# Attention stage: the instructions of a step written in another order on four engines

## What is computed

```
xn = layernorm(x)                                    # then ln1
q, k = rope(l2norm(xn @ Wq)), rope(l2norm(xn @ Wk))  # 16 heads of 8
v, clock = xn @ Wv, softplus(xn @ clock_w + clock_b)
gcp = exp(clip(cumsum(-softplus(xn @ gate_w + gate_b)), -60, 50))
p_exp = exp(p - max(p)) * clock;  p_cs = cumsum(p_exp)
q = q * gcp / (p_cs + 1e-8);  k = k / (gcp + 1e-8) * p_exp
out = softmax(causal(q @ k.T / sqrt(8))) @ v @ out_w + out_b
x1 = out + residual
y = x1 + gelu(layernorm(x1) @ mlp_w1 + mlp_b1) @ mlp_w2 + mlp_b2
x = x + layernorm(y)                                 # then the expert of each token is chosen
```

## Time and profile before

| what | value |
|---|---|
| median of three runs (lowest, highest) | 2470.77 us (2466.68, 2477.46) |
| the profiled execution: its time, its span | 2465.03 us, 2463.3 us |
| mean granted clock of TensorE over the span | 0.90 |
| `x2`, once a step: first, last of 16 | at 183.5 us, at 991.1 us |

### The profile page before, as it was taken

The page is one execution under the profiler, slowest core; times in us unless marked ns, Lnnn a source line. Parts: engine busy times, 40 slices in busy tenths (PEclk is TensorE's granted clock), DMA queues, the critical chain, the costliest instruction groups (busy, mean ns, idle before and its releaser), DMA issues. The chain is left out here.

```text
span 2463.3 us, 40082 instructions
## 1 busy us (share of the span) xinstructions
PE 1930.4 (78%) x12634; PEld 980.3 (40%) x12661; DVE 1726.9 (70%) x3563; ACT 1493.2 (61%) x2916; POOL 1102.2 (45%) x702
## 2 busy tenths in 40 slices
PE   3678887777887876199648889899888898775997
PEld 0345454444544443199612223332322222223443
DVE  4655655655656532257608999999999999994875
ACT  1576666666766653077535676666666666535875
POOL 0112111212121101158727788888888888860000
PEclk7899899999999986599878999999999999877998
DMA  3010000000100000122110000000000000003432
GB/s 136 18 31 23 23 23 23 27 23 25 37 23 19 19 14 22 31 64 85 68 39 15 25 22 22 22 21 21 21 21 21 21 30 17 18 9 101 100 82 73
DMA packets 98864, 88.51 MB, mean 36 GB/s; under 512 B 8416, under 2 KB 85392, under 8 KB 98336
## 3 DMA queue, kind: packets, MB, share of 16 engines
q1 hardware_dynamic: 91936, 68.52, 9.7%
q0 software_dynamic: 6784, 18.10, 2.2%
HBM read 38.01 MB, written 27.61 MB: 27 GB/s over the span
## 5 line engine op out<-in xcount | busy, mean ns | idle before, releaser
L1790 POOL TENSOR_TENSOR hc<-h,c_rep 128x1024 f32<-128x1024 f32 x256 | 602.1, 2361 | 179.3 <-DVE h L1772 173.1
L1772 DVE TENSOR_TENSOR_SCAN h<-decay,bank 128x1024 f32<-128x1024 f32 x256 | 585.4, 2287 | 30.3 <-DVE bank L1763 11.2
L1666 ACT ACTIVATE decay<-bank,neg_a_r 128x510 f32<-128x510 f32 x512 | 322.7, 683 | 271.5 <-PE bank L1552 271.3
L1538 PE MATMUL bank<-u_in,sel_rows 32*128 32x512 f32 x1024 | 322.8, 682 | 110.3 <-DVE h L1772 109.0
L1763 DVE TENSOR_TENSOR bank<-bank,b_rep 128x1024 f32<-128x1024 f32 x256 | 309.2, 1208 | 62.4 <-remote 51.9
L1552 PE MATMUL bank<-delta,sel_rows 32*128 32x512 f32 x1024 | 348.0, 684 | 1.5 <-ACT decay L1666 1.5
L662 ACT ACTIVATE es<-bank 128x384 f32<-128x384 f32 x512 | 210.1, 502 | 120.6 <-PE bank L467 120.5
L1011 POOL DMA_INDIRECT rows_in_dram<-row,idx x64 | 66.4, 1037 | 424.5 <-DVE row L954 409.9
L1538 PEld LDWEIGHTS bank<-u_in,sel_rows 32*128 32x128 f32 x1024 | 88.1, 195 | 306.8 <-DVE h L1772 263.9
L442 PE MATMUL bank<-xt,w_a 128*128 128x512 f32 x224 | 138.9, 713 | 70.4 <-DVE rot_b L820 32.5
L1567 PE MATMUL bank<-hc,y_sel 128*32 128x512 f32 x1024 | 151.3, 667 | 0.0
(11 more groups left out here) (334 smaller groups left out, 4185.3 us busy)
## 6 DMA issues: line engine op xcount, KB each, us to landing
r_tw<-r_o_t SPq DMA_DIRECT2D x96, 128.0 KB, 2.3
xvs<-xv SPq DMA_DIRECT2D x16, 512.0 KB, 2.9
xs<-rows_in_dram SPq DMA_DIRECT2D x72, 68.0 KB
w<-in_w_dram SPq DMA_DIRECT2D x2, 2048.0 KB
x_in<-in_x_dram SPq DMA_DIRECT2D x16, 256.0 KB
xlb_dram<-xl SPq DMA_DIRECT2D x16, 256.0 KB
xlb_m<-xlb_dram SPq DMA_DIRECT2D x16, 256.0 KB
x_m<-in_x_dram SPq DMA_DIRECT2D x16, 256.0 KB
```

Of the source, the lines that this page charges most:

```text
L1538: last = pe.matmul(BD[n % 2][:, i * STEP:(i + 1) * STEP], sel[at:at + 32, r, :], u_in[p if n < NS else q][at:at + 32, hf, :], start=True, ...
L1666: act.activation(decay[n % 4][:, i, :, 1:], seq(DL[i])[:, :, 1:], ACT.Exp, scale=c["neg_a_r"][:, hf, g:g + 1]).then_inc(s["n_da"], 1)
L1772: dve.tensor_tensor_scan(flat(h[n % RING]), decay[n % 4].rearrange("p i b t -> p (i b t)"), BD[n % 2], 0.0, ALU.mult, ALU.add).then_inc(s[ ...
L1790: pool.tensor_tensor(hc[n % RING][:, :, :], h[n % RING][:, :, :], c_rep[p][:, :].unsqueeze(1).to_broadcast([P, 2, STEP]), ALU.mult).then_i ...
```

## The change

Everything is in `attention`. No operation is added or taken out, no size and no buffer is changed, and the loop stays as it is. `stats_of`, `root`, `turned`, `heads_out` and `chain` are taken apart, so that their pieces (`bn_stats`, `bn_aggr`, `heads_rec`, `heads_o`, single activations) can stand in different places; and between the pieces now stand operations of other parts. Where two operations stood next to each other in an order that made one wait enough, the second now has its own (`f_rq` ahead of `q_t`, `f_pre0` ahead of the Abs, `r_hot` ahead of `pos`, `f_clip` ahead of `factor`).

The diff of `pe_step`, shortened:

```diff
+            if late:
+                weigh(5, k - 2, p)
+            if tail:
+                pe.wait_ge(s["m_h"], k - 2)
+                transposes(M, h_tok, s["m_ht"])
             if front:
                 pe.wait_ge(s["f_xt_sb"], k + 1)
                 since(pe, s["f_mk"], k)
                 project(FB, c["w_gate"], s["f_gate"])
             if tail:
-                pe.wait_ge(s["m_h"], k - 2)
-                transposes(M, h_tok, s["m_ht"])
+                pe.wait_ge(s["m_ht_sb"], k - 2)
+                up(0)
...
+            if late:
+                quad(6, k - 2, p)
...
             if late:
-                weigh(5, k - 2, p)
-            if tail:
-                up(3)
-
-            if late:
-                quad(6, k - 2, p)
+                back(2, k - 2)
...
+            if late:
+                back(3, k - 2)
+            if front:
+                pe.wait_ge(s["f_sq"], k + 1)
+                pe.wait_ge(s["f_ra"], k + 1)
+                pe.matmul(FA[:, :], c["ones_blk"], square[:, :], start=True, stop=True).then_inc(s["f_ssq"], 1)
+                pe.wait_ge(s["f_rb"], k + 1)
+                project(FB, c["w_k"], s["f_k"])
             if ln:
                 pe.wait_ge(s["f_xn"], k + 2)
...
             if scores:
+                weigh(3, k - 1, q)
+                quad(5, k - 1, q)
                 back(1, k - 1)
-                quad(5, k - 1, q)
```

On ACT `h_t` now comes ahead of `v_a`, `av_copy(2)` and the Abs stand between the gelus, the root of `f_vv` comes right behind the second table load, the Exp of `mag` and what follows from it come behind `exps(7)`, and `lnorm` and `neg` stand earlier or later by one group. On DVE and POOL:

```diff
-            def heads_out(i, u, par):
+            def heads_rec(i, u):
+                dve.wait_ge(s["s_tr"], u * 4 + i + 1)
+                dve.reciprocal(rec[:, :, :], AV.rearrange("q (n s w) -> q n s w", n=4, s=HS)[:, :, :, DH]).then_inc(s["s_rec"], 1)
...
+            def heads_o(i, u, par):
...
+                dve.wait_ge(s["s_rec"], u * 4 + i + 1)
...
-            if front:
-                pool.wait_ge(s["f_nb"], k + 1)
-            if tail:
+                pool.wait_ge(s["f_rs"], k + 1)
+                since(pool, s["xlb_stored"], 16 * k)
+                pool.tensor_tensor(xl[:, :, :], x_in[p][:, :, :], of_tile(mv[p][:, :, 0]), ALU.subtract).then_inc(s["f_xl"], 1)
...
-                pool.wait_ge(s["f_xl2"], k + 1)
-                pool.tensor_tensor(xl[:, :, :], xl[:, :, :], c["rows"][:, 0:1, :].to_broadcast([P, TS, D]), ALU.add).then_inc(s["f_xlb"], 1)
...
+            if front:
+                pool.wait_ge(s["f_xl2"], k + 1)
+                pool.tensor_tensor(xl[:, :, :], xl[:, :, :], c["rows"][:, 0:1, :].to_broadcast([P, TS, D]), ALU.add).then_inc(s["f_xlb"], 1)
```

More of the change, by code:

```diff
@@ L393, in since @@
                 eng.wait_ge(sem, count)
[L395 to L405, removed]
         def two_variances(dve, v, var, sem):
@@ L592, in pe_step @@
                 last.then_inc(s["m_aff"], 1)
+            if scores:
+                back(0, k - 1)
             if front:
@@ L597, in pe_step @@
             if scores:
-                weigh(2, k - 1, q)
-            if scores:
-                weigh(3, k - 1, q)
+                quad(3, k - 1, q)
             if mid:
@@ L624, in pe_step @@
                 last.then_inc(s["r_rank"], 1)
+            if scores:
+                weigh(2, k - 1, q)
+                quad(4, k - 1, q)
             if mid:
@@ L668, in av_copy, with gelu @@
                 act.activation(avs[:, :], AV[:, :], ACT.Copy).then_inc(s["s_avs"], 1)
+            def gelu(n):
+                act.wait_ge(s["m_up"], 4 * k + (n - 11))
+                act.activation(g[:, n, :], M[:, :], ACT.Gelu, bias=c["mlp_b1"][:, n:n + 1]).then_inc(s["m_gelu"], 1)
+            if tail:
+                act.wait_ge(s["m_ht"], k - 2)
+                since(act, s["m_up"], 4 * k - 12)
+                act.activation(h_t[:, :], M[:, :], ACT.Identity, scale=c["ln2_g"], bias=c["ln2_b"]).then_inc(s["m_ht_sb"], 1)
             if scores:
@@ L739, in act_step @@
                 exps(1, k - 1)
-            if tail:
-                root(vv_m[:, :, :], vv_m[:, :, :], row[q][:, :, RS0:RS1 + 1].rearrange("p j v -> p v j"), s["m_vv3"], s["m_ln3"], s["m_rs3"], k - 2)
             if front:
-                act.wait_ge(s["f_clip"], k + 1)
-                since(act, s["f_zk"], k)
-                act.activation(lgcp[:, :], cum[:, :], ACT.Exp, scale=-1.0).then_inc(s["f_gcp"], 1)
-                act.wait_ge(s["f_gcp"], k + 1)
-                act.activation(lgcp[:, :], lgcp[:, :], ACT.Ln, bias=1e-8).then_inc(s["f_lgcp"], 1)
-            if scores:
-                exps(2, k - 1)
-                av_copy(0, k - 1)
+                act.wait_ge(s["f_k"], k + 1)
+                act.wait_ge(s["f_ssq"], k + 1)
+                act.activation(square[:, :], FB[:, :], ACT.Square).then_inc(s["f_sk"], 1)
             if tail:
@@ L812, in heads_out, with bn_stats, bn_aggr @@
                     dve.tensor_tensor(o, tr[:, :, r, :, 0:DH], w, ALU.mult).then_inc(s["s_o"], 1)
-            def turned(to, bank, bank_sw, s_a, wait_a, s_b, wait_b, s_r, part):
-                if part == 0:
-                    dve.wait_ge(wait_a, k + 1)
-                    dve.tensor_tensor(seq(to), seq(bank), cos, ALU.mult).then_inc(s_a, 1)
-                    return
-                dve.wait_ge(wait_b, k + 1)
-                dve.tensor_tensor(seq(rot_b), seq(bank_sw), sin, ALU.mult).then_inc(s_b, 1)
-                dve.wait_ge(s_b, k + 1)
-                dve.tensor_tensor(to[:, :], to[:, :], rot_b[:, :], ALU.add).then_inc(s_r, 1)
+            def bn_stats(to, src, sem):
+                for j in range(TS):
+                    last = dve.bn_stats(to[:, j, :], src[:, j, :])
+                last.then_inc(sem, 1)
+            def bn_aggr(to, st, sem):
+                dve.memset(hold[:, :], 0.0)
+                for j in range(TS):
+                    last = dve.bn_aggr(to[:, j, :], st[:, j, :])
+                last.then_inc(sem, 1)
             def centred(dst, src, mean_var, rstd, sem):
@@ L839, in dve_step @@
                 centred(h_tok, x1, mv_m, rs_m, s["m_h"])
+            if ln:
+                dve.wait_ge(x_loaded[q], 16 * half + 16 * (1 + p))
+                since(dve, s["f_xl"], k)
+                bn_stats(stats, x_in[q], s["f_st"])
+                dve.wait_ge(s["f_st"], k + 2)
+                bn_aggr(mv[q], stats, s["f_mv"])
             if front:
```

343 lines of the change are left out of this document (196 added, 147 removed).

## The result

The changed kernel takes 2259.96 us, median of four runs (2257.96 to 2274.09); the kernel before, beside it, 2471.93 (2466.68 to 2477.46). The ratio is 0.916, 95% interval 0.912 to 0.919: 212 us less.

A forecast was written before the change was run, and what follows sets the result against it. The order of operations, not a full engine, was the bound. Step 44.5 us plus 1.8 for loop and clock is 46.3 against 54.8; 8.5 x 13 = 110, plus 8, 118 less: 2470.8 - 118 = 2353 us, range 2315 to 2420.

The forecast's parts named there:

- The chain through DVE: Full attention step: 14.5 us up to `x2`, 26.4 of DVE's own work, 1.2 for meeting POOL; 42.1 us.
- the overlap with POOL: POOL's two softplus operations meet DVE's scan of `cum` once a step; 0.95 to 1.57 us, taken as 1.2.
- TensorE's 43.5: Full attention step: 41.5 us of TensorE work plus the waits that stay; the larger of two bounds.
- the margin of 1.0: Full attention step: 1.0 us added for handoffs laid too tightly, giving a step of 44.5 us.
- Loop and clock: Loop branch 4.1 us in four of 13 steps, unrolled steps 1.5 in five; 1.8 us a step on average.
- the partial steps: Attention steps 0 to 2 and 16 to 18, limited by single chains; 8 us less, bounds 0 and 42.
- The excess of an unrolled step: Unrolled attention steps of the old kernel: read as about 2 us more, entered as 2.6 in five of 13.
- a step of 42.5: Low end of the forecast's full step length, whose own case of 42.5 to 47 us gave 2318 to 2387.
- B: Full attention step: margins hold and handoffs are short, 42.5 us or less; 2315 us and below; chance 0.06.
- A: POOL's other four operations drift into DVE's unbroken run, 4 to 6 us a step; 2419 us; chance 0.14.
- C: Attention's waits only move to the next count, step within 1 us; 2471 us, give or take 12; chance 0.05.
- D: Many short waits keep TensorE's clock low; at half its work at the low level 2607 us; chance 0.05.

The follow-up runs named there:

- e1: The changed kernel once more, unedited, on another chip than the first measurement; 2306.18 us, ratio 0.9211 to the kernel before.
- e13: The changed kernel again, unedited, as reference for later runs; 2307.89 us, ratio 0.9214 to the kernel before.
- e10: The changed kernel with the old order on all engines for steps up to k = 2; 2331.45 us.
- e11: The changed kernel with the old order on all engines from k = 16; 2330.42 us.
- e2: The changed kernel with one more 128x512 DVE product ahead of q's norm, in DVE's unbroken run; 2316.24 us.
- e7: The kernel before with TensorE's new list and the other engines' old lists; 2684.46 us, ratio 1.090.
- e18: The changed kernel with its loop as straight code and ScalarE's gelu table loaded right behind `v_a`; 2300.10 us, ratio 0.9163 to the kernel before.
- e14: The changed kernel with q's products with cos and sin and their add put back where they stood before; 2325.77 us.
- e5: The kernel before with one more DVE operation of about 0.6 us in front of q's `lnorm`; 2467.32 us, ratio 1.0015.
- e8: The kernel before with POOL's (GpSimd's) new list alone; 2498.71 us, ratio 1.0125.
- e9: The changed kernel with its hardware loop written out as straight code; 2303.88 us, ratio 0.9188 to the kernel before.
- e15: The changed kernel with the two last products into `rot_k` put behind the small piece that follows them; 2315.42 us.
- e4: The changed kernel with TensorE's product of `ones_blk` and q's squares made twice, ahead of the wait for `xl`; 2322.58 us.
- e17: The changed kernel with TensorE's product of `ones_blk` and k's squares made twice, behind the wait for `xl`; 2337.48 us.
- e3: The changed kernel with one more DVE reduction of a bank where DVE waits for a projection; 2306.98 us.

## Why the prediction was wrong in size

**What held.** That the order was the bound, not an engine's work. That `rot_b`, `v_a` and `avs` would stop holding TensorE, and DVE would run from `x2` to `h_tok` without a wait. The chain through DVE: 42.1 us forecast, 41.7 measured, with its parts 27.6 against 27.06 and 14.5 against 14.66. The first part is in some measure luck: DVE's own time was laid as 26.4 and was 27.06 - 2.16 = 24.9, the overlap with POOL was put at 1.2 and was 2.16, and the two errors nearly cancel. That queues and code behind attention cost nothing: the latter changed by 5.9 us, and e1 and e13, the same kernel, differ by 14 there.

**The step that failed first: TensorE's 43.5, "the larger", plus 1.0.** The busy time of 41.5 us was taken as work that stays. The same 411 matmuls are busy 39.77 us in the new order. As I read it, busy time includes the ends of pieces that a wait separates from the next, where the next matmul doesn't overlap them: a transpose of `avs` had a mean of 286 ns before and has 275 now, a matmul of a projection 615 and 593. The waits were sized well, 2.0 forecast, 1.95 measured. 39.8 + 1.95 = 41.7: both bounds of the forecast then agree with the chain, and the margin of 1.0 had nothing to cover. This cost 44.5 - 41.8 = 2.7 us a step.

**Loop and clock.** 1.8 us a step were forecast, 1.3 measured, in another split. The unrolled steps lose nothing, where 1.5 was forecast. A branch costs 47.2 - 41.8 = 5.4, not 4.1, and three of the twelve distances hold one. Its gap now lies within the last `weigh`, just ahead of the transposes of `h_tok`, and matmuls behind it run at the low level (the pair of projections 1.91 us, not 1.02):
```profile
489.55 1.08 PE L469 MATMUL bank<-es,v_a 128*32 128x256 f32 x8 [3.00 <-issue]
...
491.90 1.91 PE L430 MATMUL bank<-xt,w_a 128*128 128x512 f32 x2
```
Together 3.2 us a step over twelve steps, 38 us.

**The term that failed most: the partial steps, 8 us.** They gave 26.8 while filling, and while draining 29.9, of which 8.5 had been counted with the thirteenth full step. 8.0 + 8.5 forecast, 56.7 measured: 40 us. "Limited by single chains, so I take 8" was argued from nothing in the rows. The gate's bias, one a step, shows k = 0 to 2. Before:
```profile
82.69 0.74 DVE L842 TENSOR_SCALAR pre<-bank,vec 128x512 f32<-128x512 f32 x1
...
123.05 0.74 DVE L842 TENSOR_SCALAR pre<-bank,vec 128x512 f32<-128x512 f32 x1
165.93 0.75 DVE L842 TENSOR_SCALAR pre<-bank,vec 128x512 f32<-128x512 f32 x1
```
After:
```profile
79.44 0.72 DVE L825 TENSOR_SCALAR pre<-bank,vec 128x512 f32<-128x512 f32 x1
110.94 0.75 DVE L825 TENSOR_SCALAR pre<-bank,vec 128x512 f32<-128x512 f32 x1 [1.55 <-PE bank L430]
143.78 0.75 DVE L825 TENSOR_SCALAR pre<-bank,vec 128x512 f32<-128x512 f32 x1 [0.65 <-PE bank L430]
```
40.4 and 42.9 us became 31.5 and 32.8: these two partial steps give 8.9 and 10.0, nearly as much as a full one (54.8 - 43.1 = 11.7). They share the stalls. Even the forecast's upper bound for the partial steps, 42, was low: they gave 26.8 + 29.9 - 8.5 = 48.2. e10 and e11 confirm both ends by experiment.

With 38 and 40 on top of 118 attention comes to 196, and it gave 196.9. Steps of 41.8 with the term of 8 would have given about 2315, the range's edge; the rest is the ends'.

Two of the forecast's sums don't come out as written. The excess of an unrolled step was read as about 2 us (54.60 - 52.56) and entered as 2.6; with 2.0 the old mean has 2.0 us above the clean step, not 2.3. And a step of 42.5 gives (54.8 - 42.5 - 1.8) x 13 + 8 = 144.5 less, 2326 us, where the forecast has 2318 for it and 2315 for rival B.

**The rivals.** A did not happen: POOL's other operations stayed ahead of `x2`, as argued. But the one meeting in DVE's unbroken run that the sum did count fell on `xl` instead of the scan, and took 2.16 us instead of 1.2; it sits on the path by the 1.05 that TensorE waits. "SBUF — State Buffer" of the Trainium skill, section "SBUF: two separate sides", has one lock on a pair of ports, held for a whole instruction, between a GpSimd instruction that reads SBUF and a DVE instruction with two SBUF inputs or in a two-port mode. Here DVE instructions of 0.34 us reached 1.44, and the `row` operation of e2, with two SBUF inputs, 1.23 in place of 0.16, which agrees; whether `xl` runs in such a mode, no row here shows. B, given 0.06, is the nearest: the margins held, and a step without branch took 41.8. Its 2315 us still had the 8 for the partial steps. C fell. D did not occur here, but e7 shows that its price is real for lists that don't fit together.

**What stays open.** What a list of ACT or DVE would do alone; what slack DVE has between `xl` and `h_tok`; how much is to be had if softplus on POOL met another DVE instruction (1.05 us a step by the wait, not tried); whether e18's version is faster on a chip without the stall.

## What to carry to other kernels

Lay the new order end to end, and then believe it: take a bound from start-to-start times, since busy time read from a kernel full of waits contains ends that vanish when the waits do. Price the filling and draining steps by their own distances in the trace, one by one, before calling them single chains. To find a path that changes engine, add a little work at several places on each and look at clean steps, not totals: a total mixes in what happens at the branch. Then find the row that moved: in e14 the wait that caught the eye was not the one that cost time.

## What the runs showed of the hardware

The kernel before takes 2469 to 2472 us beside the first runs and e5 to e8, and 2504 to 2510 beside the others, on other chips. On the chip of e1 seven of the nine steps without branch have a stall behind the transposes of `h_tok` that the first profile of the same kernel lacks. TensorE, DVE and ACT stand there, GpSimd's indirect DMAs keep their pace, and the trace names no engine as the releaser of TensorE and ACT; DVE's row names TensorE. First e1, then the same place in the changed kernel's first profile:
```profile
583.67 0.78 ACT L646 ACTIVATE h_t<-bank,vec 128x512 f32<-128x512 f32 x1 [1.24 <-remote]
...
584.50 1.12 PE L485 MATMUL bank<-h_t,w_a 128*128 128x512 f32 x2 [1.53 <-issue]
```
```profile
576.95 0.76 ACT L646 ACTIVATE h_t<-bank,vec 128x512 f32<-128x512 f32 x1
...
577.76 1.12 PE L485 MATMUL bank<-h_t,w_a 128*128 128x512 f32 x2 [0.17 <-ACT h_t L646]
```
It makes 43.2 of 41.8, the straight code of e9 has it too, and it vanished in e15, where TensorE waited 1.30 for `h_tok` just there. Its cause stays open.

A branch of the hardware loop costs more than its 3 us of silence, as TensorE comes out of it at its lower clock: 5.4 on the first chip. On the chip of e1, where such a step lacks the stall, it costs 2.9 to 4.0 against its neighbours.

And one product more in TensorE's list made each branch dearer. In e4 and e17 a second idle stretch of 1.5 to 2.5 us follows the branch's gap at all three branches, and such a step costs 5.4 to 6.7 us more than its neighbours. The first profile, e1 to e3 and e10 to e15, whose TensorE lists in the loop are the changed kernel's, don't have it. What it is, the trace doesn't say.
